# Pairwise-interaction network on one core: the dots' block-diagonal operand is written by two compute engines, and each dot becomes two 64-row matmuls

## The reference

```python
e  = stack(tbl_f[ids[:, f]] for f in range(39))              # 512 x 39 x 16
x1 = einsum('bid,bjd,ijh->bhd', e, e,  W0.reshape(39, 39, 128))
x2 = einsum('bid,bjd,ijh->bhd', e, x1, W1.reshape(39, 128, 128))
z  = sum(concat([x1, x2], axis=1), axis=-1)                  # 512 x 256
h  = relu(concat([z, dense_ctx]) @ W_top1 + b_top1)          # 272 -> 512
h  = relu(h @ W_top2 + b_top2)                               # 512 -> 256
y  = h @ W_top3                                              # 512 x 1
```

## Time and profile before

| | us |
|---|---|
| median of 3 runs | 257.5 (256.31 to 258.46) |
| the profiled execution | 257.7 |
| its span | 255.9 |
| PE busy | 211.4 |
| DVE busy | 180.1 |
| ACT busy | 149.3 |
| POOL busy | 157.0 |

### The profile page before, as it was taken

One profiled execution on the slowest core, in us unless ns is written; L12 is line 12 of the kernel. 1 busy time (PEld: TensorE's weight loads), 2 busy tenths in 40 slices (PEclk: granted clock), 3 DMA queues, 4 the chain that ended last, 5 costly groups with the idle time before them and its releaser, 6 DMA issues.

```text
span 255.9 us, 3948 instructions
## 1 busy us (share of the span) xinstructions
PE 211.4 (83%) x1212; PEld 165.7 (65%) x1212; DVE 180.1 (70%) x335; ACT 149.3 (58%) x284; POOL 157.0 (61%) x165
## 2 busy tenths in 40 slices
PE   0458294971989898999898979997989799998996
PEld 0223153750766586888575868885768688876995
DVE  1497595944899979796979696969796968841000
ACT  2134254670778766776687566776876566866002
POOL 4777777777677777777777777777777750000000
PEclk9999859597699999999999999999999799999799
DMA  6200032295411202020202020202020201010000
GB/s 193 68 6 6 7 52 69 39 280 135 108 20 20 31 10 33 9 33 8 32 9 33 9 31 6 32 9 33 8 32 9 32 9 19 6 27 4 0 3 0
DMA packets 27511, 9.40 MB, mean 37 GB/s; under 512 B 22513, under 2 KB 25585, under 8 KB 27490
## 3 DMA queue, kind: packets, MB, share of 16 engines
q1 hardware_dynamic: 22370, 7.86, 13.7%
q0 software_dynamic: 5120, 1.29, 5.3%
HBM read 6.50 MB, written 0.00 MB: 25 GB/s over the span
## 4 chain that ended last, share of the span: by engine, by line
PE 42%; POOL 26%; issue 12%; DMA 9%; DVE 8%; ACT 2%; DVEq 0%; ACTq 0%; POOLq 0%
POOL gathered L348 26%; PE tower L671 10%; DMA gathered<-table,rows 8%; PE copies L622 7%; PE sums L636 4%; PE sums L637 4%; PE sums L638 4%; PE ring L660 3%; PE ring L661 2%; PE ring L662 2%; DVE turned L408 2%; DVE parts L399 1%; ACT dots L532 1%; DVE columns L442 1%; PE ring L650 1%
## 5 line engine op out<-in xcount | busy, mean ns | idle before, releaser
L348 POOL DMA_INDIRECT gathered<-table,rows x160 | 156.6, 979 | 51.7 <-issue 44.2
L428 DVE TENSOR_TENSOR prod_lo<-prod,prod_hi 128x512 fp32r<-128x512 f32 x96 | 65.0, 690 | 3.3 <-ACT prod_hi L498 3.3
L622 PE MATMUL copies<-turned,sel_sb 128*128 128x512 bf16 x112 | 42.7, 434 | 28.9 <-DVE turned L408 28.6
L420 DVE TENSOR_TENSOR prod<-first,copies 128x512 f32<-128x512 f32 x96 | 64.0, 681 | 2.8 <-ACT first L489 1.3
L498 ACT CAST prod_hi<-prod 128x512 fp32r<-128x512 f32 x96 | 58.2, 625 | 9.1 <-DVE prod L420 9.1
L671 PEld LDWEIGHTS tower<-dots,w_sb 128*128 128x128 f32 x312 | 47.7, 199 | 5.0 <-issue 0.8
L671 PE MATMUL tower<-dots,w_sb 128*128 128x128 f32 x312 | 49.8, 284 | 0.3 <-ACT dots L532 0.2
L532 ACT COPY dots<-ring 128x320 f32<-128x320 f32 x64 | 43.6, 746 | 8.0 <-PE ring L662 6.9
L636 PE MATMUL sums<-prod_hi,w_hi 128*128 128x512 f32 x96 | 47.6, 496 | 0.4 <-DVE prod_lo L428 0.2
L637 PE MATMUL sums<-prod_lo,w_hi 128*128 128x512 f32 x96 | 38.8, 404 | 0.0
L622 PEld LDWEIGHTS copies<-turned,sel_sb 128*128 128x128 bf16 x112 | 10.3, 103 | 44.0 <-DVE turned L408 33.8
(11 more groups left out here) (85 smaller groups left out, 237.8 us busy)
## 6 DMA issues: line engine op xcount, KB each, us to landing
gathered<-table,rows POOLq DMA_INDIRECT x160
diag<-columns SPq DMA_DIRECT2D x128, 20.0 KB
wt_sb<-wt SPq DMA_DIRECT2D x2, 512.0 KB
sel_f<-sel SPq DMA_DIRECT2D x1, 448.0 KB, 3.0
w0a<-w_ij SPq DMA_DIRECT2D x1, 448.0 KB, 4.4
w0b<-w_ji SPq DMA_DIRECT2D x1, 448.0 KB, 5.4
ids_sb<-ids SPq DMA_DIRECT2D x1, 85.0 KB, 2.0
ident_f<-ident SPq DMA_DIRECT2D x1, 64.0 KB, 2.8
```

Of the source, the lines that this page charges most:

```text
L348: pool.indirect_dma_start(gathered[0:n, k % NGATHER, q, :], None, table, bass.IndirectOffsetOnAxis(ap=rows[0:n, k, q:q + 1], axis=0)).then ...
L420: nc.vector.tensor_tensor(prod[:, m % NPROD, :], first[:, k % 2, :], copies[n % 3][:], ALU.mult)\
L428: nc.vector.tensor_tensor(prod_lo[:, m % NPART, :], prod[:, m % NPROD, :], prod_hi[:, m % NPART, :], ALU.subtract).then_inc(lo_ready, 1)
L622: pe.matmul(copies[n % 3][:], sel_sb[:, e, :], turned[:, k % NTURN, :], start=True, stop=True).then_inc(copied, 1)
```

## The change

- `columns`, its memsets, the large memset of `diag` and the 128 transfers of L325 are gone. `diag` now holds, for each part, 4 blocks of 40 columns instead of 8 for each sub.
- ACT writes the high part of `diag` straight from the ring bank with four activations for each block, each scaled by a column of `own_sb` (128x4, ones where the partition's sample is the b-th of its half, else zeros). DVE writes the low part with four scalar_tensor_tensor instructions (times the same scale, minus the high part). The column of ones is written once for each buffer.
- A dot over 8 samples becomes one over two times 4 samples: partitions 0 to 63 and 64 to 127 are multiplied apart, as matmuls of 64 rows and 160 columns, each into its own ring bank. One `dot` step now does two subs (12 matmuls, in turns between the two halves) and needs both ring banks; there are two such steps for each block in place of four.
- ACT still copies 128x320 four times for each block; `dots` is written in another pattern.
- SP issues the weight loads as soon as `columns_low` of blocks 0, 1 and 2 is done, and nothing more until the output. One small load (`own`) is added to the first ones.
- POOL's code is the same.

```diff
--- before
+++ after
@@ -25,6 +25,8 @@
 COLS = BLOCK * DIM
 SUB = P // DIM
 SUBS = BLOCK // SUB
+HALF = SUB // 2
+ROWS = HALF * DIM
 WIDE = FIELDS + 1
 AHEAD = 23
 TILES = 6
@@ -114,7 +116,7 @@
 STEPS = TILES + 1
 TENSOR = dict(first=-3.51, second=(-3.43, -3.32, -3.09, -2.19, -1.71, -0.56),
               tile=(-0.0, 1.0, 2.0, 3.0, 4.0, 6.0), sum_squares=5.68, columns=-0.86, x1=8.68,
-              dot=(10.74, 10.9, 11.77, 12.05))
+              dot=(10.82, 11.9))
 SCALAR = dict(first=-2.73, high=(-1.73, -1.71, -0.8, -0.66, 4.2, 4.84), squares=2.8, sums=6.9, columns=0.41,
               x1=10.57, dot=(12.12, 12.27, 13.05, 13.06))
 VECTOR = dict(product=(-4.16, -4.1, -3.16, -1.71, -1.14, -0.22), low=(-2.36, -1.86, -1.18, -0.66, 2.03, 3.28),
...
@@ -196,8 +198,8 @@
         turned_hi = sb("turned_hi", [P, 2, SUBS, P], F32R)
         turned_lo = sb("turned_lo", [P, 2, SUBS, P], F32R)
 
-        columns = sb("columns", [P, 2, SUBS, 2, WIDE], F32R)
-        diag = sb("diag", [P, 2, SUBS, 2, SUB * WIDE], F32R)
+        own_sb = sb("own_sb", [P, HALF])
+        diag = sb("diag", [P, 2, 2, HALF, SUBS, WIDE], F32R)
 
         dots = sb("dots", [P, 2, WIDE, GROUP])
         w1_sb = sb("w1_sb", [P, FIELDS, P])
...
@@ -280,7 +281,12 @@
 
         copy_order = [x for x in pe_order if x[0] in ("first", "second")]
         copy_no = {what: n for n, what in enumerate(copy_order)}
-        ring_order = [("dense", 0)] + [x for x in pe_order if x[0] in ("columns", "x1", "dot")]
+        ring_order = [("dense", 0)]
+        for what in pe_order:
+            if what[0] in ("columns", "x1"):
+                ring_order.append(what)
+            if what[0] == "dot":
+                ring_order.extend(("dot", what[1], 2 * what[2] + r) for r in range(2))
         ring_no = {what: n for n, what in enumerate(ring_order)}
         low_no = {what: n for n, what in enumerate(x for x in ring_order if x[0] in ("columns", "x1"))}
 
...
@@ -314,17 +321,9 @@
                     sp.dma_start(wt3_sb[:], wt3).then_inc(tower_in, 16)
                     sp.dma_start(bt2_sb[:], bt2).then_inc(tower_in, 16)
 
-            sp.wait_ge(zeroed, 3)
-            for k in range(BLOCKS):
+            for k in range(3):
 
                 sp.wait_ge(ring_low, low_no["columns", k] + 1)
-                if k >= 2:
-
-                    sp.wait_ge(ring_full, ring_no["dot", k - 2, SUBS - 1] + 1)
-                for b in range(SUB):
-                    sp.dma_start(diag[DIM * b:DIM * b + DIM, k % 2, :, :, WIDE * b:WIDE * b + WIDE].bitcast(F32),
-                                 columns[DIM * b:DIM * b + DIM, k % 2, :, :, :].bitcast(F32))\
-                        .then_inc(diag_in[k % 2], 16)
                 load_weights(k)
 
             sp.wait_ge(last_y, 1)
...
@@ -370,9 +369,10 @@
             nc.vector.tensor_tensor(w0_hi[QUAD:2 * QUAD, TILES, :], w0a[QUAD:2 * QUAD, TILES, :],
                                     w0_hi[QUAD:2 * QUAD, TILES, :], ALU.subtract).then_inc(ready, 1)
 
-            nc.vector.memset(diag[:].bitcast(F32), 0.0).then_inc(zeroed, 1)
-            nc.vector.memset(columns[:, :, :, 0, FIELDS:WIDE].bitcast(F32), 1.0).then_inc(zeroed, 1)
-            nc.vector.memset(columns[:, :, :, 1, FIELDS:WIDE].bitcast(F32), 0.0).then_inc(zeroed, 1)
+            nc.vector.memset(diag[:, :, 1, :, :, FIELDS:WIDE].bitcast(F32), 0.0).then_inc(marked, 1)
+            for at in range(2):
+                nc.vector.tensor_copy(diag[:, at, 0, :, :, FIELDS], own_sb[:].unsqueeze(2).broadcast_to([P, HALF, SUBS]))\
+                    .then_inc(marked, 1)
 
             def split(k, step):
 
@@ -436,11 +436,11 @@
             def columns_low(k):
                 n = ring_no["columns", k]
                 dve.wait_ge(ring_drained, n + 1)
-                if k >= 2:
-
-                    dve.wait_ge(diag_in[k % 2], 16 * SUB * (k // 2))
-                nc.vector.tensor_tensor(columns[:, k % 2, :, 1, 0:FIELDS], by_sub(ring[n % 2])[:, :, 0:FIELDS],
-                                        columns[:, k % 2, :, 0, 0:FIELDS], ALU.subtract).then_inc(ring_low, 1)
+                for b in range(HALF):
+                    low = nc.vector.scalar_tensor_tensor(diag[:, k % 2, 1, b, :, 0:FIELDS],
+                                                         by_sub(ring[n % 2])[:, :, 0:FIELDS], own_sb[:, b:b + 1],
+                                                         diag[:, k % 2, 0, b, :, 0:FIELDS], ALU.mult, ALU.subtract)
+                low.then_inc(ring_low, 1)
 
             def h1_sum(g):
 
@@ -475,9 +475,13 @@
                 act.wait_ge(ring_full, n + 1)
                 if k >= 2:
 
-                    act.wait_ge(diag_in[k % 2], 16 * SUB * (k // 2))
-                nc.scalar.copy(columns[:, k % 2, :, 0, 0:FIELDS], by_sub(ring[n % 2])[:, :, 0:FIELDS])\
-                    .then_inc(ring_drained, 1)
+                    act.wait_ge(ring_full, ring_no["dot", k - 2, SUBS - 1] + 1)
+                if k == 0:
+                    act.wait_ge(sel_in, 64)
+                for b in range(HALF):
+                    high = nc.scalar.activation(diag[:, k % 2, 0, b, :, 0:FIELDS], by_sub(ring[n % 2])[:, :, 0:FIELDS],
+                                                ACT.Identity, scale=own_sb[:, b:b + 1])
+                high.then_inc(ring_drained, 1)
 
             def store_first(k):
                 n = copy_no["first", k]
@@ -522,15 +526,15 @@
                 nc.scalar.copy(turned_hi[:, k % 2, :, :], ring[n % 2][:].rearrange("p (s h) -> p s h", h=P))\
                     .then_inc(ring_drained, 1)
 
-            def store_dots(k, s):
-                n = ring_no["dot", k, s]
-                g, at = divmod(k * BLOCK + s * SUB, GROUP)
+            def store_dots(k, part):
+                n = ring_no["dot", k, part]
+                g, at = divmod(k * BLOCK + part // 2 * 2 * SUB, GROUP)
                 act.wait_ge(ring_full, n + 1)
                 if g >= 2 and at == 0:
 
                     act.wait_ge(tower_full, NMLP * (g - 2) + 2)
-                nc.scalar.copy(dots[:, g % 2, :, at:at + SUB].rearrange("p i b -> p b i"),
-                               ring[n % 2][:, 0:SUB * WIDE].rearrange("p (b i) -> p b i", i=WIDE))\
+                to = dots[:, g % 2, :, at:at + 2 * SUB].rearrange("p i (s r b) -> p r s b i", s=2, r=2)
+                nc.scalar.copy(to[:, part % 2], ring[n % 2][:, 0:2 * HALF * WIDE].rearrange("p (s b i) -> p s b i", s=2, i=WIDE))\
                     .then_inc(ring_drained, 1)
 
             def tower_step(g, step):
...
@@ -650,16 +654,23 @@
                     mm = pe.transpose(ring[n % 2][:, P * s:P * s + P], x1[:, P * s:P * s + P], ident_f[:])
                 mm.then_inc(ring_full, 1)
 
-            def dot(k, s):
-                n = ring_no["dot", k, s]
-                pe.wait_ge(ring_low, low_no["x1", k] + 1)
-                pe.wait_ge(diag_in[k % 2], 16 * SUB * (k // 2 + 1))
+            def dot(k, pair):
+                n = ring_no["dot", k, 2 * pair]
+                pe.wait_ge(ring_low, max(low_no["x1", k], low_no["columns", k]) + 1)
+                if k < 2:
+                    pe.wait_ge(marked, 3)
                 free_ring(n)
-                to = ring[n % 2][:, 0:SUB * WIDE]
-                hi, lo = turned_hi[:, k % 2, s, :], turned_lo[:, k % 2, s, :]
-                pe.matmul(to, hi, diag[:, k % 2, s, 0, :], start=True, stop=False)
-                pe.matmul(to, hi, diag[:, k % 2, s, 1, :], start=False, stop=False)
-                pe.matmul(to, lo, diag[:, k % 2, s, 0, :], start=False, stop=True).then_inc(ring_full, 1)
+                free_ring(n + 1)
+                hi, lo = turned_hi[:, k % 2, :, :], turned_lo[:, k % 2, :, :]
+                for s in range(2):
+                    for m, (x, part) in enumerate(((hi, 0), (hi, 1), (lo, 0))):
+                        for r in range(2):
+                            rows = slice(ROWS * r, ROWS * r + ROWS)
+                            to = ring[(n + r) % 2][:, HALF * WIDE * s:HALF * WIDE * (s + 1)]
+                            mm = pe.matmul(to.rearrange("p (b i) -> p b i", i=WIDE), x[rows, 2 * pair + s, :],
+                                           diag[rows, k % 2, part, :, 2 * pair + s, :], start=(m == 0), stop=(m == 2))
+                            if s == 1 and m == 2:
+                                mm.then_inc(ring_full, 1)
 
             def second_layer(g, i):
                 if i == 0:
@@ -766,6 +777,7 @@
         "sel": sel,
         "back": back,
         "ident": np.eye(P, dtype=np.float32),
+        "own": np.kron(np.ones((2, 1), np.float32), np.kron(np.eye(HALF, dtype=np.float32), np.ones((DIM, 1), np.float32))),
         "dense": np.asarray(dense_ctx),
         "wt1": np.asarray(W_top1),
         "bt1": np.ascontiguousarray(np.asarray(b_top1).reshape(-1, P).T),
```

10 lines of the change are left out of this document (5 added, 5 removed).

## The result

| | before | changed |
|---|---|---|
| median of 4 runs each, us | 257.98 (256.31 to 259.58) | 260.25 (259.10 to 261.72) |
| ratio | | 1.0155, 95% interval [1.0101, 1.021] |
| profiled execution, its span, us | 257.7, 255.9 | 259.1, 257.3 |
| last gather begins, us | 208.1 | 208.1 |
| gathers, mean ns | 979 | 982 |

By the ratio the change makes the kernel slower by 1.6%, 4 us, where 2.5 us of gain was forecast (255.2). The medians of the table lie only 2.3 us apart; the ratio goes by fast runs alone, without those that a lower clock or a time over 1.5% above the kernel's fastest marks as slow. The time itself lies near that of the second rival (259.8: the gathers stay as they are), in part by luck: its sum was +2.1 us, and the ratio says +4.0 (2.6 to 5.4).

The account below looks back on a forecast made before the run. POOL's gathers were taken to bound the kernel until block 14, then PE. Transfers -4.6, POOL's waits -0.9, DVE +0.75, PE +0.9, +0.45 and +0.9 sum to -2.5 us, from 257.7 to 255.2; range 252.0 to 265.5.

Parts of the forecast that it names:

- the second rival: POOL's gathers: SP's transfers don't lengthen them, so the 4.6 us gain falls away; 259.8 us, chance 0.18.
- SP's 128 transfers removed: -4.6 us, the largest term and an inference.: POOL's gathers ahead of block 14: those overlapping SP's issues become shorter once the transfers go, -4.6 us; bounds 0 and -4.6.
- POOL's real waits: -0.9.: POOL after block 3: w1's load is issued earlier and delays gathers less, -0.9 us; bounds 0 and -0.9.
- DVE: +0.75.: DVE's split before the transpose: four column instructions for one, +0.75 us; in other blocks covered by its wait for the landing.
- ACT: nothing: ACT's high part: four activations for one, 0.8 us more in each block, covered by PE's other tiles, so no cost.
- the latency of transfers: nothing: Landings of `diag`: dots come a good block after their columns and PE shows no wait, so no gain.
- dots +0.9: PE's dots in blocks 12 to 14: 64-row pairs cost 1.04 against 0.9 us, +0.3 a block, +0.9 us in all.
- double bank +0.45: Block 14: the second pair waits until ACT empties both banks, with only a tile between as cover, +0.45 us.
- last block +0.9: Last block's dots until w1's matmuls: pairs and ACT's copies follow with nothing useful between, 4.7 us against 3.75, +0.9 us.
- weight loads take turns: Rival on PE's dots: the halves' loads queue, a pair costs +0.8 us and PE becomes the pace; 265.2 us, chance 0.26.
- change of form is free: Rival on PE's dots: switching between 128-row and 64-row matmuls costs nothing, -0.5 us a block; 252.8 us, chance 0.12.
- kept as it is: The clock's fall after PE's wait at block 14 was assumed unchanged; without it or with a second, about 1.7 us either way.

Follow-up runs that it names:

- the operand's work alone: Kernel before with three more scaled DVE and three more ACT instructions on each block's columns, written to an unread tile; transfers and dots unchanged: ratio 0.9984.
- the halves alone: Kernel before with only its dots replaced by pairs of 64-row halves into two banks, DMA still writing `diag`: ratio 1.0174.
- the kernel with dots by sample: Changed kernel with dots stored by sample, field innermost, so ACT writes rows instead of scattered floats: 298.3 us, ratio 1.1668.
- the two with the dense products first: Changed kernel, run twice, with the last first layer's four dense matmuls ahead of the wait for the last dots: ratios 1.0275 and 1.039, on slow chips.
- its end shared: Kernel before with the last block's dots 3 and 4 in two banks of copies, DVE copying dots 2 and 4: median 309.6 against 306.6 us, slow chip.

## Why the prediction was wrong

**The failed step: "SP's 128 transfers removed: -4.6 us, the largest term and an inference."** It was worth 0: mean 982 ns without them and 985 with them back. The 21 of 22 long gathers that overlapped an issue of SP were a coincidence of place: both stand at the same point of a block. The long gathers of the changed kernel stand there too, without SP (18 of 22 within the 5.2 us behind DVE's `columns_low`). The rival "the long gathers are not SP's doing" had said so, at 259.8, with a chance of 0.18. It deserved more, since the same list of gathers would have shown that ACT's `prod_hi` overlaps 19 of the 22, DVE's products 17 and ACT's dots 16. Nor was SP's overlap set against the short gathers: SP overlaps 40% of them and ACT's dots 29%, so that both are 2.4 to 2.5 times as frequent at the long ones, and DVE's `square_parts` 4%, against 11 of the 22.

**POOL's real waits: -0.9.** They went, as reckoned (0.9 to 0), and 0.5 came back as longer gathers; the last gather begins at 208.1 as before, and the landing of block 14 came 0.07 us sooner, so nothing of it shows.

**DVE: +0.75.** At block 14 it was 0.75, by luck, as said above; at block 13 the split takes 2.39 us for 1.38, 1.0 more. A scaled one is dearer than the plain subtract: four take 1.15 us, 0.29 each, against 0.23. The price in time is 0 within the noise (0.9984 for the work alone, at most 0.6 us), and why stays open. The cover in the other blocks was reckoned from the 2.22 us of block 14 alone, "leaves about 1 us"; at blocks 9 and 13 the wait was 1.51, and with the change none was left there.

**ACT: nothing, the latency of transfers: nothing.** Both right. The scaled activations take 405 ns, the copy that they replace 294.

**PE: dots +0.9, double bank +0.45, last block +0.9, together +2.25.** Measured +0.9 to 1.4 up to the last x1, of which 0.56 is the wait, and +1.01 behind it: +1.9 to 2.4. The mechanism and the size were right. A pair with its exit takes 0.83 us (233.32 to 234.15), and from the last x1 transposes to the first dot it is 2.37 us against 2.20 before, 0.17 for the entry: 1.00 against 0.9, where 1.04 was forecast. Six rounds of 0.107 are 0.64, which leaves the 0.2 on exit. The last block's sum put both of ACT's copies behind each pair, and so they stand (4.59 us, 4.7 forecast). The Trainium skill ("TensorEngine Tiling (Array Packing)", Key Properties) has both: the mode's change drains the engine, the tiles load and multiply in parallel. The trace agrees, with 0.17 and 0.2 us at the two changes and rounds of 0.11. The rival "weight loads take turns" is refuted by those rounds, and "change of form is free" by the 0.17 and 0.2.

**The clock: "kept as it is".** This was the second mistake. I gave "1.7 us" for another stretch and no direction, though the change adds two waits where the clock had just fallen. Ten profiles have pairs that wait for both banks (not counting the kernel with dots by sample and the two with the dense products first): six of them show 6.8 us at half clock around the end, four 3.4. The kernel before and two near it (more work on both engines; its end shared) show 3.4 to 3.7; with the wait filled there is none. These are too few to call the waits the cause. The longer stretch costs 1.6 us (20.96 against 19.38 to the end).

The sum with what was measured: 0 for transfers, gathers and DVE, +1.9 to 2.4 for PE, and 1.6 in the executions with the longer stretch: +1.9 to 4.0, where the ratio says +4.0 (2.6 to 5.4). How often it comes in the unprofiled executions isn't known. The mean granted clock of each is on record and points the same way. Worked out from it, the kernel before was 20.7 us at half clock in the mean on one chip, the operand's work alone 23.3, the halves alone 26.2, and the changed kernel with transfers back 27.5; but it doesn't say at what place, and a place where PE isn't the bound costs nothing. So the share of the clock is not settled beyond that.

## What to carry to other kernels

An overlap of long instructions with another engine's work is evidence only against all other engines' overlaps, tested the same way. Count the short instructions too, not only the long ones. When a change makes a step take two buffers where it took one, go to the place with least work between the steps: there the wait stands bare. An idle stretch of TensorE near the end can be filled with work that doesn't depend on what it waits for: here 1.1% for moving four matmuls.

## What the runs showed of the hardware

- Two matmuls of 64 rows by 160 columns, in different row halves and banks, take 0.11 us together with their fp32 weights; a 128-row matmul of 320 columns 0.15.
- A stride of 160 bytes in PE's fp32 moving operand: 432 ns a matmul of 128 columns in place of 286 with adjacent ones.
- Behind the last dots TensorE was 3.4 us at half clock in some executions and 6.8 in others, of the same kernel too (on two chips).
- A change between matmuls of 128 rows and of 64 rows: 0.17 us on entry, 0.2 on exit.
- Gathers by POOL take 949 ns alone and 979 to 985 with the other engines at work; which work does it is open. In the kernel before those that overlap DVE's `square_parts` take 1156 ns in the mean, the others 956.
- Chips differ: on some of them every kernel, before's included, took 301 to 325 us, with idle times of up to 8.2 us whose end the trace puts down to nothing.
